# First attention of a four-layer megakernel: small transfers issued by SyncE, outputs scaled five steps later, side work spread over more slots

## The reference

```python
# layer 0, attention: 16 heads, q and k of width 8, v of width 64
cp = leaky_relu(einsum('btd,dc->btc', xn, Wc.T) + bc)
q, k, v = split(cp)                       # (2, 1024, 16, 8), same, (2, 1024, 16, 64)
scores = einsum('bqhd,bkhd->bhqk', q, k) / sqrt(8)
attn = softmax(scores, axis=-1)
out = einsum('bhqk,bkhd->bqhd', attn, v).reshape(2, 1024, 1024)
s = xn + leaky_relu(einsum('btv,dv->btd', out, Wo) + bo)
x = x + s * silu(moe0(xn))
# layer 1: xn = layernorm(x); s = a linear recurrence; the gate is a mixture of 8 experts, top 2
scores = softmax(xn @ gate_w.T);  sel = top_k(scores + expert_bias, 2)
```

## Time and profile before

| | |
|---|---|
| median of 3 runs | 1419.89 us |
| the profiled execution itself | 1436.21 us, of which 1434.4 us from the first to the last instruction |
| busy over the span | PE 1156.7 (81%), DVE 948.9 (66%), POOL 772.9 (54%), ACT 609.9 (43%) |
| first attention | from about 266 to 814 us |
| of it slots 16 to 127 | without side work |
| of it about 537 to 727 us | side work beside it |

### The profile page before, as it was taken

How to read it: one execution, slowest core, us unless ns; L and a number is a source line. 1 busy time by engine, 2 the same in 40 slices (tenths; PEclk the granted TensorE clock), 3 DMA queues, 4 the chain that set the end, 5 groups by cost and what they waited for, 6 DMA issues and landing times.

```text
span 1434.4 us, 14426 instructions
## 1 busy us (share of the span) xinstructions
PE 1156.7 (81%) x4718; PEld 489.3 (34%) x4718; DVE 948.9 (66%) x1391; ACT 609.9 (43%) x877; POOL 772.9 (54%) x482
## 2 busy tenths in 40 slices
PE   5999999899999998878799786768764474669783
PEld 2444333212122212121122265546452221456372
DVE  6977563688888887888786456756654676545311
ACT  2444332466666665555466443124340221444142
POOL 0333434588878888767978503134677358652102
PEclk9999999999999999999999999879887566989797
DMA  9210200201011100000200144324210003121441
GB/s 341 86 48 26 72 23 0 65 17 40 17 43 32 30 28 28 29 28 24 91 16 24 57 133 133 104 79 131 74 40 23 29 0 115 48 96 33 130 146 46
DMA packets 77147, 90.70 MB, mean 63 GB/s; under 512 B 20528, under 2 KB 58544, under 8 KB 76848
## 3 DMA queue, kind: packets, MB, share of 16 engines
q1 hardware_dynamic: 65584, 83.11, 18.1%
q0 software_dynamic: 3072, 6.30, 1.4%
q10 hardware_dynamic: 8416, 0.36, 0.3%
HBM read 71.32 MB, written 24.77 MB: 67 GB/s over the span
## 4 chain that ended last, share of the span: by engine, by line
PE 25%; DVE 13%; POOL 11%; issue 6%; ACT 3%; DMA 1%; another core or an unknown queue 1%; ACTq 1%; POOLq 0%; SPq 0%; DVEq 0%
PE ps L133 22%; POOL ar L139 5%; PE ps L136 2%; POOL psum_sb L139 2%; DVE osb L152 2%; ACT ar L170 2%; POOL gT L183 1%; DVE ar L139 1%; DVE small L152 1%; DVE ar L152 1%; DVE small L139 1%; DVE ar L155 1%; DVE rt L139 1%; DVE ps_sb L139 1%
## 5 line engine op out<-in xcount | busy, mean ns | idle before, releaser
L133 PE MATMUL ps<-ar 128*64 128x512 f32 (+3 forms) x3052 | 684.3, 479 | 58.7 <-ACT ar L170 27.7
L133 PEld LDWEIGHTS ps<-ar 128*64 128x64 f32 (+2 forms) x3052 | 281.2, 144 | 423.5 <-issue 276.8
L170 ACT ACTIVATE ar<-ps 128x1024 f32<-128x1024 f32 (+1 forms) x286 | 284.2, 1001 | 188.3 <-PE ps L133 133.9
L152 DVE TENSOR_REDUCE small<-ps 128x2 f32<-128x1024 f32 (+1 forms) x272 | 310.3, 1156 | 65.6 <-PE ps L133 63.8
L139 POOL TENSOR_TENSOR psum_sb<-psum_sb,ar 128x1024 f32<-128x1024 f32 x128 | 305.8, 2389 | 23.7 <-ACT ar L170 9.4
L139 POOL TENSOR_TENSOR ar<-ar 128x2048 f32<-128x2048 f32 (+1 forms) x48 | 168.0, 3516 | 106.1 <-ACT ar L167 77.2
L133 PE MATMUL ps<-xnT,ar 128*128 128x512 f32 x272 | 133.5, 611 | 0.4 <-issue 0.2
L139 POOL TENSOR_TENSOR psum_sb<-ar 128x1024 f32<-128x1024 f32 x32 | 76.1, 2378 | 78.1 <-ACT ar L170 63.5
L183 POOL DMA_INDIRECT gT<-ysort,rt x32 | 31.2, 974 | 148.1 <-DMA ysort<-ar 112.5
L139 POOL TENSOR_TENSOR rec_sb<-osb,psum_sb 128x512 f32<-128x512 f32 x32 | 42.0, 1314 | 102.9 <-DVE osb L139 72.8
L155 DVE COPY ar<-ps 128x256 f32<-128x256 f32 x86 | 35.5, 416 | 76.7 <-PE ps L133 64.3
(11 more groups left out here) (148 smaller groups left out, 1248.3 us busy)
## 6 DMA issues: line engine op xcount, KB each, us to landing
ar<-in_L_w SPq DMA_DIRECT2D x30, 576.0 KB, 3.9
ar<-in_L_w SPq DMA_DIRECT2D x22, 578.0 KB, 3.7
rec_sb<-lscr SPq DMA_DIRECT2D x64, 128.0 KB, 2.8
ar<-xsort SPq DMA_DIRECT2D x52, 128.0 KB
ysort<-ar SPq DMA_DIRECT2D x52, 128.0 KB
scr<-ar SPq DMA_DIRECT2D x48, 128.0 KB, 1.9
xsort<-in_x SPq DMA_DIRECT2D x10, 512.0 KB, 12.7
ar<-scr SPq DMA_DIRECT2D x32, 112.0 KB
```

Of the source, the lines that this page charges most:

```text
L133: return self.e.matmul(o, l, r, start=start, stop=stop) if self.e else Nothing()
L152: return self.e.tensor_reduce(o, a, AX.X, op, negate=True) if negate else self.e.tensor_reduce(o, a, AX.X, op)
L170: return self.e.activation(o, a, fn, **kw) if self.e else Nothing()
```

## The change

1. ACT no longer issues transfers in the attention. The two `lcol<-lrow` transfers of a unit and the second transfer of the maxima rows (`Qs<-mT`) are issued by SP at the same slots, with the waits that ACT had.
2. The scaling moves from k = 11 to k = 16 and the projection with its addition from k = 12 to k = 17. Within a unit that is from slot 3 to slot 0 of the next unit, and from slot 4 to slot 1. `tail0` becomes (260, 266), (266, 272), (272, 274), (274, 274).
3. `LANES_B` is two lanes. Chunk 0 begins at slot 138 (134 before), `end0` with four slots a step and `ln` with three (two before); chunk 1 begins at slot 150, beside it, and `route` at slot 180 (170 before), `first` at 210 (200).

```diff
 LANES_B = [
-    [(134, "slowly", 2, "end0", 0), (0, "slowly", 2, "ln", 1, 0), (0, "slowly", 2, "end0", 1),
-     (0, "slowly", 2, "ln", 1, 1), (0, "route", 0), (0, "first", 0)],
+    [(138, "slowly", 4, "end0", 0), (0, "slowly", 3, "ln", 1, 0)],
+    [(150, "slowly", 4, "end0", 1), (0, "slowly", 3, "ln", 1, 1), (0, "route", 0), (0, "first", 0)],
 ]
 # tensor_program, unit_tail
-            if k == 12:
+            if k == 17:
 # every engine, tails
             unit_tail(x // 8 - 2, x % 8 + 8)
+            unit_tail(x // 8 - 3, x % 8 + 16)
 # every engine, tail0
-            for lo, hi in ((260, 262), (262, 269), (269, 270), (270, 272)):
+            for lo, hi in ((260, 266), (266, 272), (272, 274), (274, 274)):
 # vector_program, unit_tail
-            if k == 11:
+            if k == 16:
                 dve.wait_ge(*at(f"recip_in{m}", u))
...
-            if k == 12:
+            if k == 17:
 # scalar_program, max_rows and unit_tail
-            act.wait_ge(*at("rows", B))
-            rows_in(B, 1)
...
-                act.wait_ge(*at("lrow", u))
-                if u >= 1:
-                    act.wait_ge(*at("lsum", u - 1))
-                act.dma(lcol[:, 0:8], lrow[0:64:32, :]).then_inc(*landed(("lcol_in",)))
-                act.dma(lcol[:, 8:16], lrow[64:128:32, :]).then_inc(*landed(("lcol_in", u)))
 # sync_program
             sp.wait_ge(*at("rows", B))
-            sp.dma(Qs[48:51, s, 2 * (B % 2), :], mT[0:3, 1024 * k:1024 * k + 1024]).then_inc(*landed(("rows0_in", B)))
+            for a in range(2):
+                sp.dma(Qs[64 * a + 48:64 * a + 51, s, 2 * (B % 2) + a, :],
+                       mT[3 * a:3 * a + 3, 1024 * k:1024 * k + 1024]).then_inc(*landed((f"rows{a}_in", B)))
...
+            if k == 3:
+                sp.wait_ge(*at("lrow", u))
+                if u >= 1:
+                    sp.wait_ge(*at("lsum", u - 1))
+                sp.dma(lcol[:, 0:8], lrow[0:64:32, :]).then_inc(*landed(("lcol_in",)))
+                sp.dma(lcol[:, 8:16], lrow[64:128:32, :]).then_inc(*landed(("lcol_in", u)))
...
-                if hi == 272:
+                if lo == 274:
```

More of the change, by code:

```diff
@@ L2124, in unit_tail @@
         def unit_tail(u, k):
-            if u < 0 or u >= 32 or k != 7:
+            if u < 0 or u >= 32:
+                return
+            if k == 3:
[4 more added lines that the diff above has]
+                sp.dma(lcol[:, 8:16], lrow[64:128:32, :]).then_inc(*landed(("lcol_in", u)))
+            if k != 7:
                 return
@@ L2156, in attention @@
                 yield
+            for x in range(256, 260):
+                tails(x)
         def tail0():
-            for lo, hi in ((260, 262), (262, 269), (269, 270), (270, 272)):
+            for lo, hi in ((260, 266), (266, 272), (272, 274), (274, 274)):
                 for x in range(lo, hi):
                     tails(x)
-                if hi == 272:
+                if lo == 274:
                     sp.wait_ge(*at("acc", 31))
```

## The result

| | before | after |
|---|---|---|
| median, same chip | 1422.08 us (9 runs) | 1430.18 us (9 runs) |
| ratio | | 1.0052, 95% interval 1.0036 to 1.0067 |
| profiled execution, span | 1436.21, 1434.4 us | 1426.77, 1425.0 us |

The account below looks back on a forecast made before the run. Bound: POOL's k1 to k5, then half, maximum, half on DVE. Steady part +6.0, side work +5, end -4.7 sum to +6.3 us, so median 1419.89 becomes 1426.2; own range 1420 to 1433, overall 1404 to 1438.

Parts of the forecast that it names:

- The ring: Steady attention: POOL's k1 to k5, then DVE's half, maximum, half, set the pace; +0.43 us a pair, +6.0 over 14.
- The two shares of holding back by the old scaling: POOL's delay from the old scaling leaves: 0.3 us in the unit without rows, 0.47 in the other.
- the cast: First cast in the unit with rows, ending with the old scaling: waiting between 0 and 0.7 us, taken as 0.47.
- my count of PE's unit: PE needs about 15.1 and 16.2 us a unit against 15.35 and 16.55, fitting by 0.3 us.
- PE's stand at slot 165: Side work, last step of chunk 0's norm: PE stands 6.6 us awaiting POOL's product.
- The clock's 2.3 us: Chunk 0's norm: a lowered clock after PE's idle stretch adds 2.3 us, before the change and again at slot 165.
- the leaky products and chunk 1's small steps: Side work: chunk 0's leaky 1.9 to 0.5 us, chunk 1's 0.3 to 2.0; chunk 1's last norm step 0.9 to 3.0.
- The end: End of the attention: less ACT issuing and less PE idle before the last projection; -4.7 us (-1 to -7).
- The inversion: End of the attention: DVE inverts the last row at about 819.5 us instead of 821.64.
- PE is the bound, relief pays: Rival: PE bounds the steady pair, 1.1 us a pair go, -15.4 in all; 1400 us; chance 0.20.
- PE becomes the bound: Rival: the early projection costs PE more than its 0.3 us slack; +11 us, 1437; chance 0.22.
- The slots pay: Rival: three and four slots a step in the side work give -10 for +5; 1411 us; chance 0.18.

Follow-up runs that it names:

- e5: Changed kernel with each scaling done twice, one more DVE operation between the halves of `adds`; 1.0252 of the kernel before.
- e7: Kernel before with SyncE issuing the transfers and the second half of `adds` first in DVE's slot 0; 0.9908 of the kernel before.
- e2: Kernel before with part 2 alone (later scaling and projection), its single side-work lane starting at slot 142; 1.0089 of the kernel before.
- e9: Kernel before with parts 1 and 2, without part 3: one side-work lane from slot 142, two slots a step; 0.9992 of the kernel before.
- e12: Changed kernel with chunk 0's norm begun at slot 153 instead of 150, its last step in slot 168; 1.0015 of the kernel before.
- e8: Changed kernel with `route` begun at slot 186 instead of 180; 1.0029 of the kernel before.
- e4: Changed kernel with no edit, timed and profiled again on another chip; 1.0044 of the kernel before.
- e1: Kernel before with part 1 alone: SyncE issues the `lcol` and maxima-row transfers; 0.9952 of the kernel before.
- e10: Changed kernel with DVE's slot 0 in the order scaling, second half of `adds`, maximum; 1.0032 of the kernel before.
- e3: Kernel before with part 3 alone: two side-work lanes from slots 138 and 150, `route` at 180; 1.0054 of the kernel before.
- e6: Changed kernel with the second half of `adds` first in DVE's slot 0, ahead of maximum and scaling; 1.0253 of the kernel before.

## Why the prediction was right

**The ring.** Right. Pair 31.94 us for 31.90; the two units 15.39 and 16.55 for 15.35 and 16.55; +0.46 us a pair for +0.43 (from k1 to k1 the pair took 31.48 before). The cause is shown by `e5`, which puts more in the same place and pays all of it, and by `e7`, which takes the maximum out of it. The two shares of holding back by the old scaling came out as taken: 0.26 us for 0.3 in the unit without rows, 0.47 for 0.47 in the other, the cast, which I could only bound.

**The attribution of it.** Wrong. I gave the steady 6.0 us to part 2 and 0 to part 1, "cover being the ring". Part 2 alone costs 1.33 us a pair (`e2`), and part 1 gives 0.88 of it back once part 2 is there. Each part was costed against the kernel before, not against the kernel with the other part; the sum was right since my count of PE's unit (15.1 and 16.2 us) has no wait for ACT in it, which holds only with part 1.

**Part 1 elsewhere.** Undersized. Alone it gains 7 us (interval 4 to 10), 1 was given. The steady part is even as predicted; the rest lies in the units where the ring isn't what ends last (unit 1, the side work, the end), which my view of a steady pair did not show. In the changed kernel the first two units are 1.9 and 0.8 us shorter in its two profiles.

**Part 3.** Size right (+5 predicted; 5.5 and 6.2 by `e9` against the two profiles, 3.9 and 6.2 from unit 16 to 31 alone), composition half right. PE's stand at slot 165 came as worked out and `e12` shows that its place is the cause. The clock's 2.3 us were too much: PE worked 2.72 us at the lower level behind it, which costs it half of that, 1.4 us, since the clock was down for part of the stand already (0.55 from 606.0 to 609.8). That unit 20 took 24.77 for 24.6 all the same is luck: the first profile had the stretch at 0.58 at its start, the second did not and shows 23.33. And of the 6 to 7 us by which `e12` shortens unit 20 only 3 to 5 are net. `route`, costed at 0 with 3 either way, costs about 3.5 (5.4 less 1.9 at the end, `e8`), and the likely reason is that its stores left POOL's waiting time. These two sum to more than the 3.9 us by 2.7 (all against `e4`), so the leaky products and chunk 1's small steps must have given that back; it was not measured apart.

**The end.** -4.2 and -3.4 us for -4.7. `e1` and `e2` share it: -2.0 and -3.7; parts 1 and 2 together give -5.5 (`e9`). Up to 2 us between such lengths are the clock's. The inversion came less early than I counted (0.9 us for 2.1).

**The rivals.** "PE is the bound, relief pays" fell: 31.43 us a pair in `e1`. Less time on DVE, of which the prediction says under this head that it would be a gain were DVE the bound, gained nothing either. "PE becomes the bound" was nearer than its 0.22 said: PE waits 0.82 us for the scaling in the one unit and 0.51 in the other, and `e10` meets the second ring, which has 0.5 us of room a unit. Under its own signs it fell: k1 comes 3.02 us after k5, not later than 3.3, and no wait for the scaling is over 1 us in a steady unit. "The slots pay" fell with `e3` and `e9`: the lanes cost, alone and beside the rest.

The Trainium skill, page "SBUF — State Buffer", section "Who interferes with whom", says that such DVE and GpSimd operations exclude each other for whole instructions, by order of issue. The trace agrees: 0.67 us for a scaling issued while POOL is idle, 2.32 for one issued 0.57 us behind k1 in `e6`. In the other order, k1 issued 0.44 us behind a scaling of 0.68 us, k1 takes 2.46 us for 2.34.

## What to carry to other kernels

When two engines turn in a ring through semaphores, look for the constant gap in the timeline, and count what stands in it: 0.7 us there is 0.7 us a turn, and an operation that moves out of a busy place into the ring's idle time is not free. Before moving it, look for the next ring and its room: here that was 0.5 us a unit, so three reorderings on DVE that were each to bring about 10 us brought 6 (`e7` against `e1`), 2 to 3 (`e10`) and -30 (`e6`). Cost the parts of a change against each other, not each against the old kernel, and place side work for which an engine waits in the same step where its producer is idle anyway.

## What the runs showed that I had not expected

- A DVE operation held by POOL is recorded as busy and ends 0.54 to 0.56 us after POOL's, however long it was held: 1.75 us for a half of `adds` (`after`), 2.32 for the scaling (`e6`), both of 128x512 and both 0.68 when free.
- The granted clock differs between profiles at the same place: 0.58 and 1.00 at the start of unit 20, behind a stand of 1.97 and 1.98 us of the same kernel, and 0.73 and 1.00 between the last two projections (`e4` and `e8`). It makes 1.5 us each time.
- From the end mark to the end of the span every kernel took 584.2 to 585.2 us in the sessions where before's median was 1420 to 1422 us, and 600.4 to 603.6 in those where it was 1438 to 1439 (and in the profile of before). What differs between those chips shows there alone; its cause was not looked for.
- Two profiles of one kernel differ within the attention too, by up to 1.4 us in single units (unit 20: 24.77 and 23.33) while steady units (4 to 15) agree within 0.04.
